# The first layer's causal mask: a GpSimd select on the probabilities in place of mask products, with the value products two steps behind

## The reference

```python
q = (x @ Wq.T).reshape(Bx, Tx, H, dk)          # k and v likewise
scores = jnp.einsum('bthd,bshd->bhts', q, k) / math.sqrt(dk)
causal_mask = jnp.triu(jnp.ones((Tx, Tx), dtype=bool), k=1)
scores = jnp.where(causal_mask, jnp.float32(-jnp.inf), scores).astype(jnp.float32)
attn = jax.nn.softmax(scores, axis=-1)
out = jnp.einsum('bhts,bshd->bthd', attn, v).reshape(Bx, Tx, D)
return out @ Wo.T
```

## Time and profile before

| what | us |
|---|---|
| median of three runs | 3845.98 |
| the profiled execution | 3840.85 |
| its span | 3839.1 |
| first layer's attention, from its first loads to its last reciprocal | 108.86 to 607.16 |
| its first and last exponential begin | 159.75 and 604.89 |
| TensorE, VectorE, ScalarE, GpSimd busy over the whole span | 3039.5, 2681.6, 2180.8, 285.7 |

### The profile page before, as it was taken

How to read it: one execution, slowest core, us unless ns; L and a number is a source line. 1 busy time by engine, 2 the same in 40 slices (tenths; PEclk the granted TensorE clock), 3 DMA queues, 4 the chain that set the end, 5 groups by cost and what they waited for, 6 DMA issues and landing times. The chain is left out here.

```text
span 3839.1 us, 54232 instructions
## 1 busy us (share of the span) xinstructions
PE 3039.5 (79%) x18410; PEld 1243.4 (32%) x18410; DVE 2681.6 (70%) x5914; ACT 2180.8 (57%) x2753; POOL 285.7 (7%) x347
## 2 busy tenths in 40 slices
PE   3699996796499999996599999956339998989626
PEld 2233334342212222223355555544312222222224
DVE  5799983445599999993566666631658888888721
ACT  2266664222237777775255545522349999999602
POOL 2000000000200000000000000013120000000033
PEclk8699997898669999998699999978669999999858
DMA  6432210000422111200000000012253222220022
GB/s 228 100 54 47 47 26 2 21 0 0 164 49 36 35 29 32 40 1 5 28 1 1 1 6 3 5 52 66 74 110 53 31 31 31 31 31 1 2 72 86
DMA packets 159647, 156.48 MB, mean 41 GB/s; under 512 B 46424, under 2 KB 126056, under 8 KB 156848
## 3 DMA queue, kind: packets, MB, share of 16 engines
q1 hardware_dynamic: 155312, 145.57, 17.6%
q0 software_dynamic: 4096, 7.78, 0.6%
HBM read 91.17 MB, written 62.00 MB: 40 GB/s over the span
## 5 line engine op out<-in xcount | busy, mean ns | idle before, releaser
L1197 ACT ACTIVATE a_probs<-a_scores 128x1024 f32<-128x1024 f32 (+3 forms) x896 | 791.9, 933 | 397.4 <-PE a_scores L1094 247.6
L1220 DVE TENSOR_REDUCE a_part_max<-a_slot_ps 128x1 f32<-128x512 f32 x1280 | 798.6, 684 | 40.3 <-PE a_slot_ps L1072 38.8
L1852 DVE TENSOR_TENSOR a_probs<-a_logit_ps,a_gate 128x1024 f32<-128x1024 f32 x512 | 603.0, 1220 | 116.9 <-ACT a_gate L1805 116.9
L1072 PE MATMUL a_slot_ps<-a_k_op,a_q_op 48*128 48x512 bf16 (+3 forms) x1792 | 579.8, 380 | 113.5 <-DMA a_k_op<-scratch_k 51.6
L1811 ACT ACTIVATE a_probs<-a_probs 128x2048 f32<-128x2048 f32 x256 | 487.7, 1905 | 0.7 <-DVE a_probs L1852 0.7
L1094 PE MATMUL a_scores<-a_q_op,a_k_op 51*128 51x512 bf16 (+3 forms) x1792 | 453.2, 362 | 7.3 <-ACT a_probs L1197 6.1
L1114 PE MATMUL a_o_ps<-a_probs,a_v_op 128*32 128x512 f32 (+3 forms) x3584 | 438.0, 561 | 1.2 <-ACT a_o_sb L1184 0.6
L1072 PEld LDWEIGHTS a_slot_ps<-a_k_op,a_q_op 48*128 48x128 bf16 x1792 | 150.4, 94 | 715.5 <-DVE a_part_max L1220 468.9
L1757 PE MATMUL a_logit_ps<-a_q_op,a_k_op 96*128 96x512 bf16 x1024 | 303.5, 384 | 63.1 <-DVE a_probs L1852 51.3
L1805 ACT ACTIVATE a_gate<-a_diff_ps 128x1024 f32<-128x1024 f32 x256 | 261.2, 1020 | 60.4 <-PE a_diff_ps L1757 49.9
L1781 PE MATMUL a_o_ps<-a_probs,a_v_op 128*32 128x512 f32 x2048 | 274.5, 608 | 2.6 <-ACT a_probs L1811 2.0
(11 more groups left out here) (398 smaller groups left out, 3782.5 us busy)
## 6 DMA issues: line engine op xcount, KB each, us to landing
a_q_op<-scratch_q SPq DMA_DIRECT2D x576, 32.0 KB
a_k_op<-scratch_k SPq DMA_DIRECT2D x576, 32.0 KB
scratch_v<-p_vpad SPq DMA_DIRECT2D x16, 1024.0 KB, 4.6
a_v_op<-scratch_v SPq DMA_DIRECT2D x32, 512.0 KB, 6.4
scratch_q<-p_parts SPq DMA_DIRECT2D x24, 384.0 KB, 2.6
scratch_k<-p_parts SPq DMA_DIRECT2D x24, 384.0 KB, 2.6
a_qd_op<-scratch_g SPq DMA_DIRECT2D x192, 32.0 KB
slots<-zero_slots SPq DMA_DIRECT2D x2, 2080.0 KB, 8.7
```

Source lines behind the costliest of these rows:

```text
L1072: nc.tensor.matmul(out[:, 0:width], q_op[g][r0:r0 + MAX_ROW, e, qt * P:(qt + 1) * P], k_op[g][r0:r0 + MAX_ROW, e, kh * CH:kh * CH + width] ...
L1197: nc.scalar.activation(probs[gs % NB][:, 2 * e:2 * e + 2, off:CH], scores[e][:, :, off:CH], ACT.Exp, scale=scale).then_inc(probs_done, 1)
L1220: nc.vector.tensor_reduce(part_max[u % 2][:, kh, col:col + 1], slot[:, 0:w], axis=AX.X, op=ALU.max).then_inc(slot_done, 1)
L1852: nc.vector.tensor_tensor(probs[s % 4][:, m, :, :], logit_ps[m][:], gate[s % 2][:], op) \
```

## The change

It leaves the diagonal block of the scores unmasked, takes the exponential of all of it, and lets GpSimd overwrite the wrong side with zero by `affine_select`, in place, in the `probs` tile (4 heads by 128 columns on 128 partitions). The value products of a diagonal step wait for that (`hidden`). In the causal form values are `lag` = 2 steps behind in place of 1, and with them the copy out, the turns of outputs and `normalise` move by one step (to steps 3 and 7). The maxima's parts on GpSimd stand between the selects, in the place of step 7. In the form without a mask, `lag` is 1 and the order on each engine stays. The loads of `ident2` and `mask_b2` are gone.

```diff
-        self.lead = 6 if causal else 5
+        self.lead, self.lag = (6, 2) if causal else (5, 1)
...
-                if n == 2 and u > 0:
+                if n == self.lag + 1 and u > 0:
                     yield "o", u - 1, 1
-                if n == self.half_end[0] + 3:
+                if n == self.half_end[0] + self.lag + 2:
                     yield "o", u, 0
...
             def values(u, n):
...
                 te.wait_ge(probs_done, (u * S + n + 1) * 2)
+                if shape.diagonal(n):
+                    te.wait_ge(hidden, u * shape.diagonals(S) + shape.diagonals(n) + 1)
...
                         score(u, n, e, 1)
-                        mm = score(u, n, e, 0)
-                        if diag:
-                            mask(n, e, 1, 0)
-                            mask(n, e, 0, 0)
-                            mask(n, e, 1, 1)
-                            mm = mask(n, e, 0, 1)
-                        mm.then_inc(scores_ready, 1)
+                        score(u, n, e, 0).then_inc(scores_ready, 1)
...
-                    if n > 0:
-                        values(u, n - 1)
-                    elif u > 0:
-                        values(u - 1, S - 1)
-                    if n == 2 and u > 0:
+                    if gs >= LAG:
+                        values(*divmod(gs - LAG, S))
+                    if n == LAG + 1 and u > 0:
                         o_turn(u - 1, 1)
-                    if n == shape.half_end[0] + 3:
+                    if n == shape.half_end[0] + LAG + 2:
                         o_turn(u, 0)
...
+            def hide(u, n):
+
+                hq, kb = shape.steps[n]
+                off, gs = shape.off(hq, kb), u * S + n
+                block = probs[gs % NB][:, :, off:off + P]
+                pool.wait_ge(probs_done, 2 * gs + 2)
+                nc.gpsimd.affine_select(block, block, [[0, H], [1, P]], ALU.is_ge, zero, base=0, channel_multiplier=-1) \
+                    .then_inc(hidden, 1)
...
+            maximum_parts(0)
+            for u in range(UNITS):
+                for n in range(S):
+                    if n == S - shape.lead + 1 and u + 1 < UNITS:
+                        maximum_parts(u + 1)
+                    if shape.diagonal(n):
+                        hide(u, n)
...
-                    if n == 1 and u > 0:
+                    if n == LAG and u > 0:
                         copy_out(u - 1, 1)
-                    if n == shape.half_end[0] + 2:
+                    if n == shape.half_end[0] + LAG + 1:
                         copy_out(u, 0)
```

More of the change, by code:

```diff
@@ L925, in off, with diagonal, diagonals @@
         return max(0, kb - CPT * hq) * P if self.causal else 0
+    def diagonal(self, n):
+        hq, kb = self.steps[n]
+        return self.causal and kb >= CPT * hq
+    def diagonals(self, n):
+        return sum(self.diagonal(m) for m in range(n))
     def ahead(self, u, n):
@@ L954, in narrow_attention @@
 def narrow_attention(nc, name, shape, scale, qs, ks, vs, ctx_nat, consts, floor=None):
-    H, S, BANKS = 4, shape.n, 3
+    H, S, BANKS, LAG = 4, shape.n, 3, shape.lag
     NA = len(shape.slots)
@@ L970, in narrow_attention @@
         ident = consts["ident"]
-        ident2, mask_b2 = (sb(n, [P, 2, P], BF16) for n in ("ident2", "mask_b2"))
         mask_wide = sb("mask_wide", [P, CH])
@@ L995, in narrow_attention @@
         scores_ready, probs_done, pv_done = sem("scores_ready"), sem("probs_done"), sem("pv_done")
-        o_copied, rec_done = sem("o_copied"), sem("rec_done")
+        o_copied, rec_done, hidden = sem("o_copied"), sem("rec_done"), sem("hidden")
         block = ctx.enter_context(nc.Block())
@@ L1032, in _ @@
             if shape.causal:
-                for n, tile in (("ident2", ident2), ("mask_b2", mask_b2), ("mask_wide", mask_wide)):
-                    sp.dma_start(tile[:], consts[n]).then_inc(masks_loaded, 16)
+                sp.dma_start(mask_wide[:], consts["mask_wide"]).then_inc(masks_loaded, 16)
             load_qk(0)
@@ L1092, in score @@
                 g, off, r0, r1 = u % GROUPS, shape.off(hq, kb), jj * HALF_ROWS, jj * HALF_ROWS + MAX_ROW + 3
-                diag = shape.causal and kb >= CPT * hq
                 return nc.tensor.matmul(scores[e][:, jj, off:CH], k_op[g][r0:r1, e, kb * P:(kb + 1) * P],
[L1095 to L1102, removed]
+                                        q_op[g][r0:r1, e, hq * CH + off:(hq + 1) * CH], start=True, stop=True)
             def values(u, n):
@@ L1116, in values @@
                 mm.then_inc(pv_done, 1)
-            if shape.causal:
-                te.wait_ge(masks_loaded, 48)
             for s in range(NA):
@@ L1131, in _ @@
                     gs = u * S + n
-                    hq, kb = shape.steps[n]
-                    diag = shape.causal and kb >= CPT * hq
                     for e in range(2):
@@ L1158, in _ @@
                         max_turn(u + 1)
-            values(UNITS - 1, S - 1)
+            for gs in range(UNITS * S - LAG, UNITS * S):
+                values(*divmod(gs, S))
             o_turn(UNITS - 1, 1)
@@ L1165, in _, with maximum_parts @@
             pool.wait_ge(pool_step, 1)
-            for u in range(UNITS):
+            zero = nc.gpsimd.to_reg(0.0)
+            def hide(u, n):
[5 more added lines that the diff above has]
+                    .then_inc(hidden, 1)
+            def maximum_parts(u):
                 out = max_parts[u % 2]
@@ L1206, in _ @@
                 dve.wait_ge(preset, 2)
-                dve.wait_ge(masks_loaded, 48)
+                dve.wait_ge(masks_loaded, 16)
             def a_slot(u, s):
@@ L2574, in four_layers @@
         descending = {n: sb(f"descending{n}", [P, n]) for n in (16, EXPERTS)}
-        consts |= {n: a[n] for n in ("one_rows", "ident2", "mask_b2", "mask_wide")}
+        consts |= {n: a[n] for n in ("one_rows", "mask_wide")}
         ident = consts["ident"]
@@ L2674, in four_layers @@
                 switch_experts(nc, "f3e", x, weights, sent, slots[1], results[1], ident, None, out)
-def halves(m):
-    return np.tile(m.reshape(2, HALF_ROWS, P).transpose(1, 0, 2), (2, 1, 1))
 def shape_constants():
@@ L2699, in shape_constants @@
         "one_rows": np.ones((3, 2 * T), bf16),
-        "ident2": halves(np.eye(P)).astype(bf16),
         "mask_wide": np.concatenate([np.zeros((P, CH - P)), np.where(i[None] > i[:, None], NEG, 0)], 1).astype(np.float32),
-        "mask_b2": halves(np.where(i[:, None] > i[None], NEG, 0)).astype(bf16),
         "select": select.astype(bf16),
```

## The result

| | before | after |
|---|---|---|
| median of four runs each, us | 3848.63 | 3878.91 |
| lowest to highest | 3845.41 to 3851.53 | 3873.75 to 3882.85 |
| ratio of the times, with its 95% interval | | 1.0078 (1.0061 to 1.0096) |
| the profiled execution, and its span | 3840.85, 3839.1 | 3878.34, 3876.6 |
| first layer's attention, last reciprocal at | 607.16 | 636.31 |

The change costs 30 us. The forecast was 3851, its range 3838 to 3866, and the result lies above the range. Of the 37.5 us between the two profiled executions, 29.15 lie ahead of the last reciprocal of the first layer's attention: 1.94 less before the first exponential, 1.7 more in the first unit, 26.7 in the 13 units after it and 2.7 in the end stretch. The other 8.3 lie behind the attention, where both kernels run the same code.

A forecast was written before the change was run, and what follows sets the result against it. VectorE's 25.9 us of reductions plus 2.56 us idle bound each unit; lag +7, start -0.9, first unit -1.0 and end -0.3 made +4.8 us, forecast 3851 by the median of 3845.98, range 3838 to 3866.

The forecast's parts named there:

- clean unit: One steady unit of the first layer's attention at granted clock 1.00; forecast to go from 28.48 to 29.0 us.
- the places: VectorE's idle places at steps 0, 2, 3, 6, 7, 8, 9 and 10; forecast sum 2.95 us a unit, 2.45 before.
- no gain from the mask products as such: Steady units: mask products stand where TensorE waits for VectorE's bank anyway, so removing them gains about 0.1 us a unit.
- Rival B: Steady units: TensorE's stream is the bound, so removing masks takes out VectorE's 2.56 us idle a unit; 3808; chance 0.10.
- The +7 for the lag: Steady units: value products and turns at other steps add 0.50 us a unit, over some 14 units +7 us.
- The first exponential: Start: two loads go, so the first product waits less: -0.9 us.
- The first unit: Its first two steps have no values, so VectorE's 1.32 us idle at 165.43 shrinks: -1.0 us, bounds -1.3 and +0.8.
- The end stretch: Last one and a half units, TensorE on the path: masks -3.1, wider values +1.5, last select +1.3; together -0.3 us.
- The last select: End of the attention: it stands bare on the path, +1.3 us.
- Not decisive: the select: GpSimd, diagonal steps: 1.27 us for each select, hidden by the second step of lag with 3.0 us of slack.
- Rival C: GpSimd: selects are long, 3.56 us each, and its queue becomes the bound; +24 us, 3870; chance 0.08.
- Rival D: Selects and VectorE's masked reductions exclude one another; 5.1 us lost a unit, +76 us, 3922; chance 0.04.

The follow-up runs named there:

- kernel 2: The kernel before with value products two steps behind and nothing else, masks still by products, no select: 3867.59 us, ratio 1.0039.
- 6: The kernel before with the turns of outputs moved from steps 2 and 6 to steps 4 and 11: 3840.12 us, ratio 0.9981.
- kernel 3: The kernel before without its mask products and nothing in their place, one step of lag: 3861.13 us, ratio 1.0032.
- kernel 1: The changed kernel (select, two steps of lag) with the mask products put back, redundantly: 3863.23 us, ratio 1.0041.
- kernel 4: The changed kernel with score products made twice: in steps 0, 1, 4 and 5, 3862.35 us, ratio 1.0038; in steps 4 and 5 only, 3870.95, ratio 1.0059.
- kernel 7: The kernel before with turns at steps 4 and 11, short masked slots first, and the select for the masks at one step of lag: 3823.83 us, ratio 0.9934.
- 5: The changed kernel with value products one step behind instead of two, the select kept: 3856.97 us, ratio 1.0024.

## Why the prediction was wrong

**Right: what bounds the unit.** VectorE's reductions plus its idle places. The clean unit came out at 29.09 for 29.0 forecast, with the places at 0.20 (0.1 to 0.2), 0.58 (0.52), 0.37 (0.37), 0.57 (0.55), 0.25 (0.27), 0.52 (0.52), 0.31 (0.31) and 0.10 (0.21). Kernels 2 (0.65 us more, 0.5 forecast) and 6 (turns moved: 0.61 less, 0.7 forecast) confirm the method on both sides of zero.

**Right: no gain from the mask products as such.** 0.1 us a unit was forecast, 0.11 (kernel 3) and 0.10 (kernel 1 less after) measured at full clock. Rival B, faster, fell with it.

**Wrong, the step that failed: "So in the steady part the masks are worth about 0.1 us a unit, not 6."** It holds at one clock level only. I had read the clock of 1.00 beside TensorE's 26.66 us and took it as given. It hung on the work that I was taking out. With 25.4 of 29.1 us the clock fell in 11 of 13 units, and 18.9 us of their 26.7 came by that. The sum had no term for the clock and no rival had it, so the range could not hold the result. By the medians, lag and select with all masks in place (kernel 1) make +16 of the +30, their own falls included, and taking the masks out makes the other half: a saving of work turned into a loss. The +7 for the lag failed by the same missing term. At full clock it was in order, 8.4 in the 13 units; measured alone (kernel 2) it is 11.7 in them, 15.8 with the first unit and the end, and 15 to 20 of the whole by ratio and by medians.

**Wrong, smaller: the first unit and the end.** The first exponential came 1.9 us sooner (0.9 forecast). The first unit took 30.92 us, not 28.2 (29.24 before, less the 1.0 forecast): the clock of 0.50 that it starts at lasted to 170.8 instead of 164.8. VectorE's 1.32 us of idle time at 165.43 did not go but became 1.67 at 165.34 and 1.08 at 168.49. The Trainium skill (TensorE: Matmul & The Clock Gate, Part 1) says that the throttled clock is the resting state and that activity releases it; before and after, less work and a later rise, agree with that. The other profiles don't settle what delays it: the rise is at 168.9 with the lag alone (kernel 2) and at 178.1 with the masks out alone (kernel 3), but at 174.9 with products added (kernel 4) and at 165.5 without masks in kernel 7. The end stretch took 2.7 us more (0.3 less forecast), with the clock at 0.93 where it had been 1.00. With the masks in and the lag (kernel 2) it takes 2.2 more, where wider values had been put at 1.5; with the masks out alone, and no fall there, 1.5 less (kernel 3), where 3.1 had been forecast for them. The last select, put at 1.3, makes its value products wait 0.22.

**Not decisive: the select.** 0.637 us measured, 1.27 taken. Rival C (a long select) fell: no value product waits for one but the last unit's, 0.22 us. The Trainium skill's lower figure (GPSIMD Engine Reference, Elementwise), an estimated 0.8 us, is close to it; by its figure for branching bodies, an estimated 5.1 us, a select would be eight times longer than measured. The about 6 us that its section on instruction dispatch adds for a first call are not seen: the first select, at 160.26, took 0.64 us like the rest. Rival D (the engines exclude one another) fell: VectorE's busy time a unit is 26.11 with selects (kernel 1) and 26.11 without (kernel 2).

**Open.** What picks the units and the places of the falls (after, two of 13 units have none), and whether it is how much TensorE has to do or also when. Why with one step of lag and no masks the falls are few and long, and with two steps many and short. The start of the first unit, as said. And behind the attention, where all run the same code, the profiled executions lie up to 16 us apart, the kernel before's being the shortest; so differences between whole profiled executions are not used above, only stretches of the attention and medians.

## What to carry to other kernels

Work on TensorE while another engine sets the pace may be what keeps the clock up, and taking it off was worth only 0.1 us a unit here, so a forecast needs a rival in which the granted clock falls, priced by the products on the path. Here such work came out at no loss only together with the pacing engine's idle time (kernel 7). And price a rearrangement by the pacing engine's idle places one by one: here that was good to 0.1 us a unit.

## What was unexpected of the hardware

TensorE's clock can fall to half in the middle of a stretch in which it is busy most of the time and never idle for long: after, ahead of the fall at 232.25, TensorE is busy for 5.32 of 6.20 us, and its longest gap there is 0.42. Its longest in the 7 us ahead of any of the 11 falls is 0.42 too.

```profile
226.00:232.20 6.20, 5.32 (x47) 1.73 (x43) 5.77 (x18) 4.77 (x6) 0.00 (x0) 1.00 0.67 87
...
231.99 0.28 PE L1079 MATMUL a_slot_ps<-a_k_op,a_q_op 48*128 48x256 bf16 x1 [0.42 <-DVE a_part_max L1226]
232.80 1.93 PE L1115 MATMUL a_o_ps<-a_probs,a_v_op 128*32 128x512 f32 x8
```

A fall costs about a third of a us for each us that it lasts after, and about a quarter in kernels 3 and 5, in units bound by VectorE. By the timelines above, of what TensorE does at half speed only what stands between two slots (value products, turns) makes VectorE wait. And products that compute nothing new (kernel 4) gave back more than half of the loss.
